# Sums, statistics and convolution tiles in another order on VectorE, in a four-block network on one Trainium2 core

## The reference

```python
x = layernorm(x + mamba_and_mlp(x))     # L0_attn
x = layernorm(x + moe_top2_dense(x))    # L0_ffn
x = layernorm(x + attention(x))         # L1_attn, 16 heads, relative positions
x = layernorm(x + moe_top2_capacity(x)) # L1_ffn
```

```python
zxbcdt = rmsnorm(x) @ in_proj_w.T             # z 256, xBC 512, dt 4
xBC = silu(causal_conv(xBC, 4 taps) + conv_b)
# state-space recurrence over the 1024 tokens, here in 8 chunks of 128
x1 = x + mixer_scale * mamba(...)
h = rmsnorm(x1)
out = x1 + mlp_scale * ((silu(h @ gate_w.T) * (h @ up_w.T)) @ down_w.T)
```

## Time and profile before

| | us |
|---|---|
| median of 3 runs (lowest, highest) | 1363.65 (1363.63, 1367.66) |
| the profiled execution: time | 1364.65 |
| its span, first to last instruction | 1362.9 |
| PE busy | 1224.1 (90% of the span) |
| DVE busy | 1091.9 (80%) |
| ACT busy | 902.2 (66%) |
| POOL busy | 295.2 (22%) |
| mean granted TensorE clock | 0.967 of full speed |

### The profile page before, as it was taken

How to read it: one execution, slowest core, us unless ns; L and a number is a source line. 1 busy time by engine, 2 the same in 40 slices (tenths; PEclk the granted TensorE clock), 3 DMA queues, 4 the chain that set the end, 5 groups by cost and what they waited for, 6 DMA issues and landing times. The chain is left out here.

```text
span 1362.9 us, 39431 instructions
## 1 busy us (share of the span) xinstructions
PE 1224.1 (90%) x16528; PEld 648.2 (48%) x16528; DVE 1091.9 (80%) x2184; ACT 902.2 (66%) x1739; POOL 295.2 (22%) x417
## 2 busy tenths in 40 slices
PE   4988888889888778999999999999999999994995
PEld 2555445545554423555555444454445544432552
DVE  6777888989785888999999989989899998934123
ACT  5665345537513305999998888888889888891242
POOL 2222131330312015000000200601106011054471
PEclk9999989999898988999999999999999999996998
DMA  5080000200208503102122011302111200011235
GB/s 144 1 234 16 1 2 17 111 2 1 112 1 154 144 1 146 38 21 45 36 56 64 21 37 45 83 27 61 38 44 40 63 13 22 13 43 39 58 101 187
DMA packets 59703, 77.72 MB, mean 57 GB/s; under 512 B 15010, under 2 KB 41189, under 8 KB 57686
## 3 DMA queue, kind: packets, MB, share of 16 engines
q1 hardware_dynamic: 56454, 70.95, 19.4%
q0 software_dynamic: 3072, 4.25, 1.0%
HBM read 37.18 MB, written 40.03 MB: 57 GB/s over the span
## 5 line engine op out<-in xcount | busy, mean ns | idle before, releaser
L1491 ACT ACTIVATE space<-ps 128x512 f32<-128x512 f32 x1024 | 605.4, 598 | 85.9 <-PE ps L671 37.3
L2151 DVE TENSOR_REDUCE smax<-ps 128x1 f32<-128x1024 f32 x512 | 613.6, 1220 | 50.6 <-PE ps L671 26.0
L671 PE MATMUL ps<-space 96*32 96x512 bf16 (+2 forms) x8432 | 614.9, 381 | 23.3 <-DVE smax L2151 12.8
L671 PEld LDWEIGHTS ps<-space 96*32 96x32 bf16 (+2 forms) x8432 | 255.0, 98 | 286.6 <-DVE smax L2151 42.6
L1052 PE MATMUL ps<-space 128*9 128x256 f32 x4096 | 319.6, 379 | 0.0
L1052 PEld LDWEIGHTS ps<-space 128*9 128x9 f32 x4096 | 119.8, 92 | 98.1 <-ACT space L1491 1.0
L1355 ACT ACTIVATE btok<-ps 128x128 f32<-128x128 f32 x32 | 8.9, 278 | 106.1 <-issue 89.6
L2096 DVE SCALAR_TENSOR_TENSOR x<-ps,gsel,x 128x128 f32<-128x128 f32 x256 | 69.0, 342 | 8.0 <-PE ps L671 7.6
L671 PE MATMUL ps<-w_exp,xnT 128*128 128x512 f32 x128 | 63.5, 620 | 13.3 <-DVE x L2096 13.3
L1596 POOL TENSOR_SCALAR eps_sum<-mv 128x4 f32<-128x4 f32 x32 | 7.4, 233 | 314.0 <-DVEq L1867 313.3
L671 PE MATMUL ps<-ones,ident 128*128 128x512 bf16 x228 | 59.0, 419 | 17.4 <-POOLq L1707 12.3
(11 more groups left out here) (250 smaller groups left out, 1416.5 us busy)
## 6 DMA issues: line engine op xcount, KB each, us to landing
head_sums<-space SPq DMA_DIRECT2D x31, 256.0 KB
q_rows<-space SPq DMA_DIRECT2D x24, 256.0 KB, 2.5
k_rows<-space SPq DMA_DIRECT2D x24, 256.0 KB, 2.8
space<-k_rows SPq DMA_DIRECT2D x16, 384.0 KB, 5.4
space<-q_rows SPq DMA_DIRECT2D x16, 384.0 KB, 7.1
expert_out<-x_all SPq DMA_DIRECT2D x2, 2048.0 KB, 18.3
space<-expert_out SPq DMA_DIRECT2D x4, 1024.0 KB, 9.5
v_rows<-space SPq DMA_DIRECT2D x4, 576.0 KB, 3.4
```

Of the source, the lines that this page charges most:

```text
L671: return nc.tensor.matmul(out, lhsT, rhs, start=first, stop=last)
L1491: nc.scalar.activation(prob[:, QUAD * (step % PROB_SETS) + unit % QUAD, :], bank(STB + unit % 2), ACT.Exp)\
L2151: v.tensor_reduce(smax[:, N % 2, i:i + 1], ps[:, b0:b0 + 2, :].rearrange("p k n -> p (k n)"), AX.X, ALU.max).then_inc(S.s_max, 1)
```

## The change

On VectorE `statistics` is taken out of `skip_sum`; `skip_rows` moves into the MLP's rounds, ahead of the last hidden product's round (behind `hidden` of n = 6). Behind the rounds the order is: the first convolution tile left over, both sums, chunk 0's inputs, both statistics, the second tile, the keys, the third tile, the values, chunk 0's weights. On ScalarE the SiLU of the second tile stands behind the tail's second half, then the queries, the SiLU of the third tile, the load of the exponential's table and chunk 0's exponential. In slots without left-over tiles ScalarE's order stays as it was (there the table load has its old place); VectorE's sums, inputs and statistics change their order there too. TensorE, GpSimd and SyncE keep their programs.

```diff
@@ ScalarE @@
-                if m is not None:
-                    for j in range(min(conv_in_mlp(q), 2 * HID_TILES - 1), N_CONV):
-                        silu_conv(m, j)
-                table_of(ACT.Exp, 1)
+                late = list(range(min(conv_in_mlp(q), 2 * HID_TILES - 1), N_CONV)) if m is not None else []
+                if late:
+                    silu_conv(m, late[0])
+                if len(late) <= 1:
+                    table_of(ACT.Exp, 1)
...
                     evac_half("tail", q, 1, 6, scale=ln_g[:], bias=ln_b[:])
+                if len(late) > 1:
+                    silu_conv(m, late[1])
+                if q is not None:
+                    evac_queries(q)
+                if len(late) > 1:
+                    silu_conv(m, late[2])
+                    table_of(ACT.Exp, 1)
                 if m is not None:
                     chunk_exp(m, 0)
-                if q is not None:
-                    evac_queries(q)
@@ VectorE @@
                 dve.wait_ge(S.skip_sum, 2 * b + H + 1)
-                statistics(xa, H, 0)
...
                     if p is not None:
                         hidden(p, n)
+                    if p is not None and n == 2 * HID_TILES - 2:
+                        skip_rows(p)
...
-                if m is not None:
-                    for j in range(conv_in_mlp(q), N_CONV):
-                        convolve(m, j)
+                late = list(range(conv_in_mlp(q), N_CONV)) if m is not None else []
+                if late:
+                    convolve(m, late[0])
                 if m == 0:
                     position_parts(1)
-                if p is not None:
-                    skip_rows(p)
                 if p is not None:
                     for H in range(2):
                         skip_sum(p, H)
                 if m is not None:
                     chunk_inputs(m, 0)
+                if p is not None:
+                    for H in range(2):
+                        statistics(xa, H, 0)
+                if late:
+                    convolve(m, late[1])
                 if q is not None:
                     for H in range(2):
                         evac_keys(q, H)
-                if m is not None:
-                    chunk_weights(m, 0)
+                if late:
+                    convolve(m, late[2])
                 if q is not None:
                     for H in range(2):
                         evac_values(q, H)
+                if m is not None:
+                    chunk_weights(m, 0)
```

## The result

| | before | after |
|---|---|---|
| median (lowest, highest) of 15 runs each, us | 1364.52 (1362.33, 1367.66) | 1370.38 (1367.57, 1372.59) |
| ratio to before, with its 95% interval | | 1.0045 [1.0033, 1.0057] |
| the profiled execution: time, span, us | 1364.65, 1362.9 | 1370.45, 1368.7 |
| DVE, ACT busy, us | 1091.9, 902.2 | 1091.2, 902.4 |

The kernel became slower by 0.45%, 4.5 to 7.8 us by the interval. The engines do the same work; what was added is waiting.

What follows compares the result with a forecast made beforehand. No engine is full; a chain between engines, mostly VectorE's order of work, bounds it. 1.9 + 2.85 + 0.7 + 1.4 = 6.85 us on 1364.65 gives 1371.5, less 1.0 for the median: 1370.5 us, 8 in 10 range 1364.5 to 1374.5.

Steps and rivals of the forecast that it cites:

- The sum of 6.85 us: Whole kernel: 1.9 + 2.85 + 0.7 + 1.4 us added to the profiled execution's 1364.65, giving 1371.5.
- The 1.0 that was taken off for the median: Whole kernel: the median of the runs shown lay 1.0 below the profiled time, so 1370.5 us was predicted.
- Slot 1: First carry: late statistics delay GpSimd's roots and so chunk 0's decays, +1.9 us, bounds 0.5 and 3.1.
- my upper bound: Slot 1, 3.1 us: TensorE, waiting for the same decay, falls to 1.2 GHz for the first chunk's products.
- Slot 2: First carry: waits for sums, late SiLUs and the table load ahead of chunk 0's exponential, 239.3 against 236.44, +2.85 us.
- Slot 3: First carry at 353.3 against 352.54, where VectorE had waited 4.90 us for the keys at lower clock: +0.7 us.
- TensorE's clock: Slots 2 and 3: last key product at 1.2 GHz after a longer pause, +0.7 each, 1.4 us in all, bounds 0 and 2.6.
- The shift is passed on: Chunk loops behind the first carry: a shift of that carry was taken as a shift of the whole rest.
- the rival that they would: Chunk loops swallow half of the 5.45 us without the clock: 1366.4 us, chance 0.13.
- Slot 4: The first half's statistics, 1.50 us, fall into VectorE's 2.34 us wait for the keys' products: 0 us.
- The rival of the filled holes: Slots 2 and 3: ScalarE not in the way, VectorE's work sets the carry, gains 0.3 and 2.4: 1360.9 us, chance 0.09.
- some 0.6 more in each loop: Chunk loops of slots 2 and 3: extra time in the clock term's upper bound of 2.6 us.

Runs made afterwards that it cites:

- decays_first: The changed kernel, but GpSimd makes chunk 0's decays of slot 1 ahead of the two inverse roots; ratio to before 1.0025 [1.0011, 1.0038].
- clock_kept: The changed kernel with 20 idle-filling matmuls on TensorE in slot 1 between chunk 0's carried and state products; ratio to before 1.0024 [1.0013, 1.0036].
- queries_first: The changed kernel, but ScalarE evacuates the queries ahead of the second late tile's SiLU; ratio to before 1.0035 [1.0021, 1.0048].
- table_again: The changed kernel with ScalarE's tables switched twice more ahead of chunk 0's exponential in slots 2 and 3; one run, 1377.44 us.
- slot1_only: The changed kernel with VectorE's new order in slot 1 alone, the other slots and ScalarE as before; ratio to before 1.0014 [0.9998, 1.0030].
- slots234_only: The changed kernel with the new order in slots 2, 3 and 4 and slot 1 as before; ratio to before 1.0030 [1.0019, 1.0042].
- refilled: Before's kernel reordered: residual early, two late tiles and first statistics in the down products' waits, queries before third SiLU, decays before roots; 1354.04 us, ratio 0.9913.
- residual_only: The kernel before with only the residual x + x1 moved ahead of the last hidden product, in all slots; ratio to before 0.9972 [0.9959, 0.9985].
- two_tiles_first: The changed kernel with the second late tile beside the first, ahead of the sums, its SiLU likewise; ratio to before 1.0010 [0.9996, 1.0025].

## Why the prediction was right, point by point

The time was forecast at 1370.5 and came out at 1370.38; the direction and the places were right, but a hit by 0.12 is luck. The sum of 6.85 us was 1.05 too high for the profiled execution (1371.5 against 1370.45). The 1.0 that was taken off for the median came from three runs of before; over fifteen that median is 0.13 below its profiled time and not 1.0, and this error made up for the other. Laid out by the landmarks, with what the lag behind before was at each:

| landmark | lag | added | forecast |
|---|---|---|---|
| slot 1, first carry | 2.85 | 2.85 | 1.9 |
| slot 2, last hidden product (219.00) | 2.88 | 0.03 | 0 |
| slot 2, first carry (241.96) | 5.52 | 2.64 | 2.85 + 0.7 |
| slot 3, last hidden product (336.15) | 6.05 | 0.53 | 0 |
| slot 3, first carry (359.11) | 6.57 | 0.52 | 0.7 + 0.7 |
| slot 4, keys (457.09) | 6.82 | 0.25 | 0 |
| end of the span (1368.7) | 5.8 | -1.0 | 0 |

- **Slot 1** was right in its mechanism: taking chunk 0's decays ahead of the roots gives the whole lag back (decays_first), and VectorE alone waits for nothing else. Its size was too small, 1.9 for 2.85. The root's start moved by 1.96, near the 2.12 worked out. What I missed lies between: from the root's start to the carry it is 3.87 us instead of 2.98. The root's first step took 0.77 us instead of 0.23, at a place where it runs beside VectorE's weights (see the last section). The 0.45 saved at hdec doesn't reach the carry in full, because what ends last is no longer hdec (124.70) but TensorE's state product (125.40), which runs at the lower level; without that it would be some 0.5 us earlier (clock_kept). The clock was in my upper bound and not in the sum.
- **Slot 2**: +2.64 for +2.85. Every wait came as laid out: 1.02 and 2.92 ahead of the sums (forecast 1.1 and 2.9), the queries behind a SiLU, 1.50 ahead of the weights (forecast 1.5). The two places named as causes, ScalarE's order ahead of the queries and of the exponential, are shown by queries_first (-1.89) and table_again (the load counts in full).
- **Slot 3**: +0.52 for +0.7. But the reason that I gave for the difference to slot 2 needs a limit: the 22.44 of before is no property of the slot. slot1_only has it in slot 2. The forecast of 0.7 was read off one execution of before that had the low stretch in slot 3; without it the same order of work would have added some 2.6 there, as in slot 2.
- **TensorE's clock**, +1.4 for the last key products in slots 2 and 3, is the term that failed: they took 1.12 and 1.13 us, after pauses of 2.95 and 2.96. But in slot 3 the level did fall, just behind the key product. By TensorE's timeline of the changed kernel, the values' products in slots 2 and 3:

```profile
235.46 1.95 PE L671 MATMUL ps<-w_qkv,xnT 128*128 128x128 f32 x16
...
352.62 3.45 PE L671 MATMUL ps<-w_qkv,xnT 128*128 128x128 f32 x16
```

The granted clock is 1.00 from 234 to 239 us and 0.66 from 351.5 to 356.5. The 1.5 us more lie beside VectorE's third tile, as the prediction had it, and cost nothing. Five kernels have this pause (after, slots234_only, decays_first, clock_kept, table_again), in ten places. In seven of them the level fell; in three of these it fell behind the key product and was free, in four it caught the product, which took 2.07, 1.31, 1.62 and 2.08 us. These four are what the slots were longer by (0.94, 0.19, 0.5 and 0.95). So the fall was foreseen rightly more often than not, but its price hangs on whether it comes ahead of one product or behind it. Its mean over the ten is 0.26, and a term of 0.3 each would have been fair.
- **The shift is passed on.** The lag of slot 1 stood in full at slot 2's last hidden product, 93.5 us later (93.45 before, 93.48 after). In the eleven profiles this stretch takes 93.1 to 94.5 us and doesn't get shorter with the lag. So the loops swallowed nothing, to about 1 us, and the rival that they would is out.
- **Slot 4**: nothing, as said. VectorE waits 0.92 us for the keys instead of 2.34; the 0.25 came earlier, by slot 4's first hidden product (425.79 before, 432.59 after).
- **The rival of the filled holes** fell as argued, at ScalarE: VectorE ended the values at 239.85, the exponential started 0.9 us later, at 240.74, and the weights waited 1.50 for it. It was not wrong as an idea. With the queries ahead and the tiles in the holes that are really there, it is refilled, and some 12 us faster than before.

The terms that were too small (slot 1, 0.95; the stretches between, 0.8), those too large (clock 1.4, slots 2 and 3 0.4) and the last 1.0 us, which belongs to no changed part and is within what that stretch varies by, leave the 1.05 named above.

The 0.53 between slot 2's carry and slot 3's last hidden product arose in slot 2's chunk loop. The lag is 5.51 us at the second carry (241.00 and 246.51), 5.84 at the third (248.29 and 254.13) and 6.26 at the fourth (254.62 and 260.88); 0.2 of it is gone again by slot 3. Busy time in the two stretches about these carries, as in the earlier trace rows, before and then after:

```profile
245.00:250.00 5.00, 4.70 (x75) 2.93 (x75) 3.96 (x12) 2.42 (x4) 1.68 (x3) 0.67 0.54 205
250.00:255.00 5.00, 5.00 (x28) 3.40 (x28) 4.86 (x16) 4.32 (x9) 2.73 (x2) 0.99 0.27 106
...
250.50:255.50 5.00, 4.69 (x74) 3.76 (x75) 3.54 (x11) 2.14 (x3) 1.19 (x2) 0.50 0.54 204
255.50:260.50 5.00, 5.00 (x22) 2.73 (x21) 4.90 (x15) 4.11 (x10) 3.22 (x2) 0.83 0.16 61
```

TensorE was at its lower level there for longer than before (granted clock 0.50 and 0.83, against 0.67 and 0.99), and VectorE waited for it. That is the "some 0.6 more in each loop" of the prediction's upper bound, in one of two loops. Whether the change brings it is not shown: the same stretch took 93.66 us before and 95.30 in slot1_only, with the same order in slot 2, and 93.43 in decays_first with the new one.

## What to carry to other kernels

Before work is moved into a wait, look at what the work had been filling: here the late tiles and the first statistics lay in the wait for the down products, and moving them away cost more than the wait for the keys was worth. In queues that work in order, follow each moved instruction to the other engines: a SiLU that waits for a late tile, put ahead of an evacuation that was ready, and two small roots ahead of a decay, once their input came late, held up the whole core. And here the carried chain passed a lag on in full, so that such places could be judged by one landmark each, more sharply than by the time of the run; several executions would be needed to tell the clock's part from the order's.

## What the runs showed of the hardware

- A switch of ScalarE's table costs 1.50 us from one tiny activation to the next with a load between (table_again), and 1.42 (before) or 1.43 (after) from a SiLU's end to an activation behind load and tiny activation. The Trainium skill (ScalarE: Activation LUTs, section on what ACT_TABLE_LOAD costs) has the same 1.28 us for the load, and a drain of some 1.38 us that is not seen here.
- TensorE's lower level followed the same pause of 2.95 us in seven of ten places, in four of them at once and in three only behind the next product. In before and in slot1_only it fell in one of two slots behind a pause of 2.37 us; in residual_only, behind 1.1 us, in none. Twenty filling matmuls kept the granted clock at 1.00 (clock_kept).
- GpSimd's addition on 128x4 took 0.76 to 0.78 us instead of 0.23 where VectorE's product for the weights or a convolution tile ran beside it: 121.65 beside 121.64 in the changed kernel, 121.96 in decays_first for both, and 230.96 beside a tile from 230.88. In two_tiles_first, where VectorE stands still at that place of slot 2, it took 0.23, by GpSimd's timeline:

```profile
231.53 0.23 POOL L1600 TENSOR_SCALAR eps_sum<-mv 128x4 f32<-128x4 f32 x1 [0.16 <-POOL rstd L1602]
```

hdec's 1.06 us in the earlier trace rows, instead of 0.61, fits this too: it started at 121.58, while VectorE's weights ran (121.26 for 0.91 us).
